# Expert layer with eight routed experts: gate and up products with the weights as the stationary operand

## The chip, the cores and the metric

The kernel runs on one core of a Trainium2 chip, in one launch. The metric is the device time of that launch in microseconds (us), as the median of several runs. All arithmetic of the stage in question is f32.

## What is computed

The reference normalises a batch of 4 x 1024 tokens of 256 features, adds a causal attention with 16 heads and a mixture of experts to the input, and returns the sum. The change touches the experts alone. Each token goes to the 2 of 8 experts that its router logits choose. An expert is a gated layer:

```
w_gate = transpose(gating_einsum, (0, 3, 1, 2)).reshape(E, F, 2 * H)        # E=8 experts, F=256, H=256
gate_out = ragged_dot(sorted_xs, w_gate, group_sizes)                       # gate and up in one product
activation = gelu(gate_out[:, 0, :]) * gate_out[:, 1, :]
expert_outputs = ragged_dot(activation, linear, group_sizes)                # down, 256 -> 256
out = sum over the token's 2 experts of weight * per_expert_scale * expert_outputs
```

## The kernel before, in words

The program is a row of stages that end in a barrier each: `project` (layer norm, q, k, v), `route` (which token goes to which expert), `attend`, `experts`, `combine` (weights the expert rows, projects the context, adds all up). The route stage sorts the 8192 pairs of token and expert into `NST` = 72 tiles of 128 rows; a tile belongs to one expert, whose number stands in `tile_expert`, in memory, because it depends on the data.

In `experts` each tile s passes through these steps, every one on its own engine, tied by semaphores:

- POOL gathers the tile's 128 rows of 256 numbers from memory by an indirect DMA (`gather`, L951) into one of `RR` = 4 buffers, 6 tiles ahead.
- TensorE (PE) transposes them in two 128x128 pieces (`rows_T`, L1028), and ACT copies the result out of PSUM (`xT_copy`, L981).
- `gate_up` (L1037): two matmuls of 512 columns into one PSUM bank, one for each half of the 256 features. The stationary operand is the transposed tile (128x128), the moving one are the expert's 512 columns of gate and up weights, addressed with the expert number read by `expert_of` (L1032, `value_load`). The result has tokens on the partitions.
- ACT computes the gelu of the gate half (`gelu`, L985), VectorE (DVE) multiplies it by the up half (L1014, `hid`).
- PE transposes `hid` in two pieces (`hidden_T`, L1044) and DVE copies them out of PSUM (L1016, `hT`).
- `down` (L1050): two matmuls of 256 columns, stationary `hT`, moving the expert's down weights, again by the expert's number.
- ACT copies the result out (`store`, L990), and POOL scatters the 128 rows to memory (`scatter`, L956).

One f32 matmul, and its weight load, shows as two records each in the trace; a transpose shows as one of each.

PE's order is written out by hand in `turn`: two reads of expert numbers, `hidden_T(s-1)`, `rows_T(s+1)`, `down(s-2)`, `gate_up(s+1)`. PE and ACT run a hardware loop (`Fori`) over four tiles a pass, DVE one over two; POOL's instructions are written out without a loop. PSUM and SBUF tiles between the engines are double buffered. SP (the DMA queue) loads the down weights (2 MB) and the first inputs of `combine` (over 4 MB) at the start of the stage, L936 to L943.

Of the kernel before, what the change touches and what calls it, by code (L numbers as in the profile page):

```python
# [894 lines left out]
def experts(nc, ins, scratch, keep, last_weights):  # L895
# [4 lines left out]
    with ExitStack() as ctx:  # L900
# [8 lines left out]
        hid = sb("hid", [P, 2, HID])  # L909
# [4 lines left out]
        hp = ctx.enter_context(nc.psum_tensor("hp", [P, 2, CH], F32))  # L914
# [7 lines left out]
        gu_ready, gate_ready, hid_ready = sem("gu_ready"), sem("gate_ready"), sem("hid_ready")  # L922
        hp_ready, hT_ready = sem("hp_ready"), sem("hT_ready")
        yp_ready, y_ready = sem("yp_ready"), sem("y_ready")
        block = ctx.enter_context(nc.Block())

        def tiles(eng, body):

            with eng.Fori(0, NST // 2) as i:
                for par in range(2):  # L930
                    body(2 * i + par, par, i)
# [44 lines left out]
        @block.scalar  # L976
        def _(act):

            def xT_copy(s, par):
                act.wait_ge(tp_ready, s + 1)  # L980
                act.activation(xT[:, par].rearrange("p a t -> p (a t)"), tp[:, par, 0:D], ACT.Copy).then_inc(xT_ready, 1)  # L981

            def gelu(s, par):
                act.wait_ge(gu_ready, s + 1)
                act.activation(gate[:, par], gu[:, par, 0:HID], ACT.Gelu_apprx_tanh).then_inc(gate_ready, 1)  # L985

            def store(s, m):
                act.wait_ge(yp_ready, s + 1)
                act.wait_ge(y_free, s + 1)
                act.activation(y[:, m], yp[:, m % 2, 0:D], ACT.Copy).then_inc(y_ready, 1)  # L990

            xT_copy(0, 0)
            gelu(0, 0)
            xT_copy(1, 1)
            gelu(1, 1)
            xT_copy(2, 0)
            with act.Fori(0, NST // RR - 1) as i:
                for j in range(RR):
                    s = RR * i + 2 + j
                    gelu(s, j % 2)  # L1000
                    xT_copy(s + 1, 1 - j % 2)
                    store(s - 2, j)
            for s in range(NST - 2, NST + 2):
                if s < NST:
                    gelu(s, s % 2)
                if s + 1 < NST:
                    xT_copy(s + 1, (s + 1) % 2)
                store(s - 2, (s - 2) % RR)
# [12 lines left out]
        def _(pe):  # L1021
            pe.wait_ge(keep["w_gu_in"], 16 * NE)

            def rows_T(s, m, i):

                pe.wait_ge(rows_in[m], 16 * (i + 1))
                for dh in range(DH):
                    last = pe.transpose(tp[:, m % 2, dh * P:(dh + 1) * P], rows[:, m, dh * P:(dh + 1) * P], keep["ident"][:, :])  # L1028
                last.then_inc(tp_ready, 1)

            def expert_of(s):
                return pe.value_load(keep["tile_expert"][0:1, ds(s, 1)], min_val=0, max_val=NE - 1)  # L1032

            def gate_up(s, par, e):
# [12 lines left out]
            def down(s, par, e):  # L1047
                pe.wait_ge(hT_ready, s + 1)
                for dh in range(DH):
                    last = pe.matmul(yp[:, par, 0:D], hT[:, par, dh], w_down[:, ds(e * DH + dh, 1)].rearrange("p a c -> p (a c)"),  # L1050
# [3 lines left out]


            rows_T(0, 0, 0)
            gate_up(0, 0, expert_of(0))
            rows_T(1, 1, 0)
            gate_up(1, 1, expert_of(1))
            hidden_T(0, 0)  # L1060
            rows_T(2, 2, 0)
            gate_up(2, 0, expert_of(2))
            pe.wait_ge(w_in, 16 * NE)

            def turn(s, j, i):

                coming, going = expert_of(s + 1), expert_of(s - 2)
                hidden_T(s - 1, (j + 1) % 2)
                rows_T(s + 1, (j + 1) % RR, i + (j + 1) // RR)
                down(s - 2, j % 2, going)  # L1070
                gate_up(s + 1, (j + 1) % 2, coming)

            with pe.Fori(0, NST // RR - 1) as i:
                for j in range(2, 2 + RR):
# [274 lines left out]
```

## Time and profile before

| what | value |
|---|---|
| time, median of 3 runs | 939.3 us (938.69, 939.3, 1016.51) |
| time of the profiled execution | 941.12 us |
| its span, first to last instruction | 939.4 us |
| stage `experts`, in the span | about 632 to 879 us |
| PE busy in the whole span | 812.5 us, 86% |
| DVE, ACT, POOL busy | 562.1, 483.2, 390.0 us |
| mean granted clock of PE | 0.937 of full speed |

The time of the profiled execution is 1.7 us above its span, which is what lies around the first and the last instruction. Times in rows are microseconds from the start of the span unless marked ns. PE busy counts matmuls, whose ends are modelled and overlap the next one's start; the distance from start to start is the firmer number. "PEld" is PE loading its stationary operand, "q" behind an engine's name its queue of register and semaphore instructions.

### The profile page before, as it was taken

How to read it: one execution, taken by the hardware profiler on the slowest of the kernel's cores; microseconds unless marked ns; L12 is line 12 of the kernel's file. 1: busy time of each engine (PE TensorE's matmuls, PEld its weight loads, DVE VectorE, ACT ScalarE, POOL GpSimd, SP SyncE). 2: the span in 40 equal slices, each digit the busy share in tenths (PEclk: the TensorE clock that was granted, in tenths of full speed). 3: DMA queues.
4: the chain of work that ended last, by engine and by line, in shares of the span. 5: the costliest groups of instructions: out<-in, count | busy, mean ns of one | idle time of the engine just before them, and what ended most of it. 6: DMA issues, size and time to landing. Idle time of an engine off the chain costs nothing. (4 is left out here: it accounts for less than half of the span.)

```text
span 939.4 us, 17505 instructions
## 1 busy us (share of the span) xinstructions
PE 812.5 (86%) x5618; PEld 426.3 (45%) x5619; DVE 562.1 (60%) x1560; ACT 483.2 (51%) x1011; POOL 390.0 (42%) x456
## 2 busy tenths in 40 slices
PE   5989601799999999999999999856999999999598
PEld 2555400134444444444444444313555656555497
DVE  4767364988888888888888888301222222222177
ACT  2333300067777777777777777852333333333374
POOL 3545340033223233322323332323666666665398
PEclk9999855589999999999999999996999999999799
DMA  4999899295555666555566600009222222222485
GB/s 157 221 263 269 213 107 121 34 253 74 62 61 57 82 81 81 67 62 61 59 82 81 81 3 3 2 6 321 86 84 84 84 84 84 84 85 78 129 245 182
DMA packets 115004, 100.32 MB, mean 107 GB/s; under 512 B 58172, under 2 KB 95676, under 8 KB 114876
## 3 DMA queue, kind: packets, MB, share of 16 engines
q1 hardware_dynamic: 105976, 80.50, 46.9%
q0 software_dynamic: 8960, 18.95, 6.4%
q8 instruction: 37, 0.61, 0.3%
q14 instruction: 31, 0.25, 0.1%
HBM read 63.89 MB, written 35.00 MB: 105 GB/s over the span
## 5 line engine op out<-in xcount | busy, mean ns | idle before, releaser
L784 ACT ACTIVATE probs<-spsum 128x512 f32<-128x512 f32 x576 | 312.1, 604 | 169.6 <-PE spsum L835 163.8
L742 DVE CUSTOM_DVE_ANT_0 junk<-mpsum,mask 128x128 bf16<-128x128 f32 (+7 forms) x512 | 360.0, 754 | 58.5 <-issue 51.7
L824 PE MATMUL mpsum<-ks,qs 102*128 102x512 bf16 (+3 forms) x768 | 183.5, 343 | 45.9 <-DVE cpsum L731 26.3
L722 POOL TENSOR_SCALAR_AFFINE_SELECT probs<-probs 128x512 f32<-128x512 f32 x128 | 78.8, 634 | 340.8 <-ACT probs L784 340.8
L835 PE MATMUL spsum<-qs,ks 105*128 105x512 bf16 (+3 forms) x768 | 199.2, 329 | 10.6 <-ACT probs L784 8.3
L855 PE MATMUL cpsum<-probs,vs 128*17 128x256 f32 (+2 forms) x2560 | 152.7, 360 | 1.5 <-POOL probs L722 0.8
L1037 PE MATMUL gu<-w_gu,xTs 128*128 x288 | 139.2, 607 | 1.7 <-ACT xTs L981 1.7
L1016 DVE COPY hT<-hp 128x256 f32<-128x256 f32 x72 | 30.6, 425 | 167.8 <-PE hp L1044 100.6
L824 PEld LDWEIGHTS mpsum<-ks,qs 102*128 102x128 bf16 x768 | 69.8, 100 | 122.5 <-DVE maxima L742 39.8
L835 PEld LDWEIGHTS spsum<-qs,ks 105*128 105x128 bf16 x768 | 67.1, 97 | 102.9 <-ACT probs L784 52.9
L956 POOL DMA_INDIRECT expert_rows<-y,places x72 | 70.7, 983 | 72.2 <-ACT y L990 42.2
L855 PEld LDWEIGHTS cpsum<-probs,vs 128*17 128x17 f32 x2560 | 59.8, 97 | 77.4 <-issue 36.4
L951 POOL DMA_INDIRECT rows<-xn_rows,places x72 | 69.3, 962 | 34.9 <-issue 20.7
L985 ACT ACTIVATE gate<-gu 128x256 f32<-128x256 f32 x72 | 27.7, 384 | 100.7 <-issue 64.0
L1050 PE MATMUL yp<-w_down,hT 128*128 x288 | 74.2, 380 | 0.4 <-issue 0.4
L1037 PEld LDWEIGHTS gu<-w_gu,xTs 128*128 128x128 f32 x288 | 52.1, 193 | 45.4 <-issue 38.5
L712 POOL DMA_INDIRECT slot_map<-entries_now,slots x64 | 61.8, 966 | 17.2 <-issue 17.2
L417 PE MATMUL qkpsum<-xT,w_qk 128*128 128x512 f32 x128 | 59.8, 612 | 4.4 <-DVE rest L359 3.3
L1014 DVE TENSOR_TENSOR hid<-gu,gate 128x256 f32<-128x256 f32 x72 | 30.2, 420 | 49.3 <-ACT gate L985 49.3
L1050 PEld LDWEIGHTS yp<-w_down,hT 128*128 128x128 f32 x288 | 49.1, 190 | 4.6 <-issue 0.9
L312 POOL TENSOR_TENSOR parts<-rest,parts 128x512 bf16<-128x512 f32 x32 | 37.0, 1157 | 32.0 <-DVE parts L361 32.0
L990 ACT ACTIVATE y<-yp 128x256 f32<-128x256 f32 x72 | 27.7, 384 | 36.2 <-issue 31.8
(124 smaller groups left out, 698.5 us busy)
## 6 DMA issues: line engine op xcount, KB each, us to landing
qk_parts<-parts SPq DMA_DIRECT2D x32, 384.0 KB, 4.4
qs<-qk_parts SPq DMA_DIRECT2D x96, 128.0 KB
ks<-qk_parts SPq DMA_DIRECT2D x96, 128.0 KB
yk<-expert_rows SPq DMA_DIRECT2D x32, 256.0 KB, 3.1
v_rows<-vt SPq DMA_DIRECT2D x32, 136.0 KB, 4.5
vs<-v_rows SPq DMA_DIRECT2D x16, 272.0 KB, 12.0
x_in<-in_x SPq DMA_DIRECT2D x8, 512.0 KB, 6.3
xn_rows<-xn SPq DMA_DIRECT2D x8, 512.0 KB, 5.8
```

Source lines behind the costliest of these rows:

```text
L417: last = pe.matmul(qkpsum[:, q % 2], w_qk[:, dh, q], xT[:, par, dh], start=dh == 0, stop=dh == DH - 1)
L712: pool.indirect_dma_start(scratch["map"], bass.IndirectOffsetOnAxis(ap=slots[:, par, k, i:i + 1].bitcast(U32), axis=0), entries[:, par, k, ...
L722: pool.affine_select(out=part, in_=part, compare_op=ALU.is_ge, fill=0.0, base=0, pattern=[[0, 4], [1, P]], channel_multiplier=-1).then_inc ...
L742: last = dve.tensor_tensor_reduce(junk[:, slot, c:c + w], mpsum[:, slot, c:c + w], keep["mask"][:, S - w:S], 1.0, 3 * NEG, ALU.add, ALU.ma ...
L784: act.activation(probs[:, u % PRING, h], spsum[:, (4 * u + h) % SRING], ACT.Exp, scale=SCALE).then_inc(exp_done, 1)
L824: last = pe.matmul(mpsum[:, slot, at + c:at + e], qs[hq][0:R_MAX, h, qt * P:(qt + 1) * P], ks[hq][0:R_MAX, h, c:e], start=True, stop=True)
L835: last = pe.matmul(spsum[:, (4 * u + h) % SRING, c:c + w], ks[hq][:, h, kt * P:(kt + 1) * P], qs[hq][:, h, q0:q0 + w], start=True, stop=True)
L855: last = pe.matmul(cpsum[32 * h:32 * h + VW, q0 % CH:q0 % CH + w], vs[hq][:, kt, h], probs[:, u % PRING, h, c:c + w], start=i == 0 and (u, ...
L951: pool.indirect_dma_start(rows[:, s % RR], None, scratch["xn"], bass.IndirectOffsetOnAxis(ap=places[:, s, 0:1].bitcast(U32), axis=0)).then ...
L956: pool.indirect_dma_start(scratch["y"], bass.IndirectOffsetOnAxis(ap=places[:, s, 1:2].bitcast(U32), axis=0), y[:, s % RR], None).then_inc ...
L1037: last = pe.matmul(gu[:, par], xT[:, par, dh], w_gu[:, ds(e * DH + dh, 1)].rearrange("p a c -> p (a c)"), start=dh == 0, stop=dh == DH - 1)
L1050: last = pe.matmul(yp[:, par, 0:D], hT[:, par, dh], w_down[:, ds(e * DH + dh, 1)].rearrange("p a c -> p (a c)"), start=dh == 0, stop=dh == ...
```

## The change

The gate and up products are turned round: the expert's weights are the stationary operand, and the transposed tile moves. The product then comes out with the hidden units on the partitions, which is what `down` wants as its stationary operand, so `hidden_T`, its PSUM tile `hp` and the copy out of it are gone, and DVE's multiply writes `hT` itself. Each tile has 8 matmuls of 128 columns in place of 2 of 512. The stationary operand is read from `w_now`, a double-buffered copy (128 x 1024 numbers) of the expert's weights, which DVE makes for each tile with an expert number that it reads itself; PE waits for it with a new semaphore. All loops are written out, addresses of expert numbers are constants, and PE's order is `gate_up(s)`, `rows_T(s+2)`, `down(s-1)`, one read of an expert number. ACT's order is `gelu(s)`, `xT_copy(s+2)`, `store(s-1)`. `down` has an explicit wait on `y_ready`. POOL and SP are as before.

```diff
-        hid = sb("hid", [P, 2, HID])
+        w_now = sb("w_now", [P, 2, DH, 2 * HID])
-        hp = ctx.enter_context(nc.psum_tensor("hp", [P, 2, CH], F32))
...
         @block.scalar
-            with act.Fori(0, NST // RR - 1) as i:
-                for j in range(RR):
-                    s = RR * i + 2 + j
-                    gelu(s, j % 2)
-                    xT_copy(s + 1, 1 - j % 2)
-                    store(s - 2, j)
...
+            xT_copy(0)
+            xT_copy(1)
+            for s in range(NST):
+                gelu(s)
+                if s + 2 < NST:
+                    xT_copy(s + 2)
+                if s >= 1:
+                    store(s - 1)
+            store(NST - 1)
 
         @block.vector
         def _(dve):
-            def body(s, par, i):
+            def weights(s):
+
+                e = dve.value_load(keep["tile_expert"][0:1, s:s + 1], min_val=0, max_val=NE - 1)
+                dve.tensor_copy(w_now[:, s % 2].rearrange("p a c -> p (a c)"), w_gu[:, ds(e * DH, DH)].rearrange("p a c -> p (a c)")).then_inc(w_ready, 1)
+
+            dve.wait_ge(keep["w_gu_in"], 16 * NE)
+            weights(0)
+            weights(1)
+            for s in range(NST):
                 dve.wait_ge(gate_ready, s + 1)
-                dve.tensor_tensor(hid[:, par], gu[:, par, HID:2 * HID], gate[:, par], ALU.mult).then_inc(hid_ready, 1)
-                dve.wait_ge(hp_ready, s + 1)
-                dve.tensor_copy(hT[:, par].rearrange("p a t -> p (a t)"), hp[:, par, 0:HID]).then_inc(hT_ready, 1)
-
-            tiles(dve, body)
+                dve.tensor_tensor(hT[:, s % 2].rearrange("p a t -> p (a t)"), gu[:, s % 2, HID:2 * HID], gate[:, s % 2], ALU.mult).then_inc(hT_ready, 1)
+                if s + 2 < NST:
+                    weights(s + 2)
 
         @block.tensor
...
+            def gate_up(s):
+
                 pe.wait_ge(xT_ready, s + 1)
+                pe.wait_ge(w_ready, s + 1)
+                for c in range(2 * HID // P):
+                    for dh in range(DH):
+                        last = pe.matmul(gu[:, s % 2, P * c:P * (c + 1)], w_now[:, s % 2, dh, P * c:P * (c + 1)],
+                                         xT[:, s % 2, dh], start=dh == 0, stop=dh == DH - 1)
+                last.then_inc(gu_ready, 1)
+
+            def down(s, e):
+                pe.wait_ge(hT_ready, s + 1)
+                if s >= 2:
+                    pe.wait_ge(y_ready, s - 1)
                 for dh in range(DH):
-                    last = pe.matmul(gu[:, par], xT[:, par, dh], w_gu[:, ds(e * DH + dh, 1)].rearrange("p a c -> p (a c)"),
-                                     start=dh == 0, stop=dh == DH - 1)
-                last.then_inc(gu_ready, 1)
-
-            def hidden_T(s, par):
-                pe.wait_ge(hid_ready, s + 1)
-                for dh in range(DH):
-                    last = pe.transpose(hp[:, par, dh * P:(dh + 1) * P], hid[:, par, dh * P:(dh + 1) * P], keep["ident"][:, :])
-                last.then_inc(hp_ready, 1)
...
-            with pe.Fori(0, NST // RR - 1) as i:
-                for j in range(2, 2 + RR):
-                    turn(RR * i + j, j, i)
...
+            rows_T(0)
+            rows_T(1)
+            going = expert_of(0)
+            for s in range(NST):
+                gate_up(s)
+                if s + 2 < NST:
+                    rows_T(s + 2)
+                if s == 1:
+                    pe.wait_ge(w_in, 16 * NE)
+                if s >= 1:
+                    down(s - 1, going)
+                    going = expert_of(s)
+            down(NST - 1, going)
```

## Rows read from the trace of the kernel before

**Rows 1.** Windows by stage: window, us, each engine's busy us, PEclk, DMA share, GB/s

```profile
653.60:867.80 214.20, 211.79 (x829) 127.11 (x829) 53.88 (x138) 79.52 (x207) 131.32 (x135) 1.00 0.27 87
879.00:939.40 60.40, 53.17 (x320) 47.93 (x320) 39.65 (x96) 35.35 (x80) 47.56 (x32) 0.90 0.70 210
```

**Rows 2.** Timeline of one turn: start, us, engine, line, operation, tiles [idle before]

```profile
672.12 0.38 PE L1044 MATMUL hp<-ident,hid 128*128 128x128 f32 x2
...
672.32 0.38 ACT L985 ACTIVATE gate<-gu 128x256 f32<-128x256 f32 x1 [1.33 <-issue]
672.34 0.38 PE L1028 MATMUL tp<-ident,rows 128*128 128x128 f32 x2
...
672.54 0.42 DVE L1016 COPY hT<-hp 128x256 f32<-128x256 f32 x1 [2.26 <-issue]
672.55 0.96 POOL L951 DMA_INDIRECT rows<-xn_rows,places  x1 [0.30 <-issue]
672.56 1.03 PE L1050 MATMUL yp<-w_down,hT 128*128 x4
672.76 0.39 ACT L981 ACTIVATE xTs<-tp 128x256 f32<-128x256 f32 x1
672.92 0.42 DVE L1014 TENSOR_TENSOR hid<-gu,gate 128x256 f32<-128x256 f32 x1
...
673.42 1.88 PE L1037 MATMUL gu<-w_gu,xTs 128*128 x4
673.62 0.38 ACT L990 ACTIVATE y<-yp 128x256 f32<-128x256 f32 x1 [0.48 <-issue]
...
674.28 0.98 POOL L956 DMA_INDIRECT expert_rows<-y,places  x1 [0.77 <-issue]
...
675.14 0.38 PE L1044 MATMUL hp<-ident,hid 128*128 128x128 f32 x2
```

**Rows 3.** Timeline of PE: a late turn, and the turns of hidden units 1 and 70

```profile
653.58 0.44 PE L1044 MATMUL hp<-ident,hid 128*128 128x128 f32 x2
...
678.49 0.43 PE L1044 MATMUL hp<-ident,hid 128*128 128x128 f32 x2 [0.17 <-issue]
...
867.81 0.38 PE L1044 MATMUL hp<-ident,hid 128*128 128x128 f32 x2
```

**Rows 4.** Timeline of weight loads, in two narrow windows, and of eight transposes in `combine`

```profile
681.89 0.19 PEld L1050 LDWEIGHTS yp<-w_down,hT 128*128 128x128 f32 x1
...
681.89 0.30 PEld L1050 LDWEIGHTS yp<-w_down,hT 128*128 128x128 f32 x2
...
903.96 1.04 PE L1164 MATMUL sumsT<-ident,ctxT 128*128 128x128 f32 x8
```

**Rows 5.** One line's instructions: count, ns min/median/max, first and last start

```profile
L1032 PEldq TENSOR_LOAD <-tile_expert x144: 295/302/494, 640.5 to 870.0; - x144
...
L1050 PEldq FUSED_REGOPS  x144: 55/60/60, 653.9 to 870.9; - x144
```

**Rows 6.** DVE copies: a row of groups by shape (busy, mean ns), and one line's durations

```profile
L346 DVE COPY xT<-tpsum 128x512 f32<-128x512 f32 x8 | 5.5, 685 | 1.9 <-PE tpsum L404 1.9
...
L361 DVE CAST parts<-rest x32: 426/428/886, 18.3 to 107.5; 128x512 bf16<-128x512 f32 x32
```

**Rows 7.** Timeline in `project`: a DVE cast beside a POOL instruction

```profile
42.35 1.16 POOL L312 TENSOR_TENSOR parts<-rest,parts 128x512 bf16<-128x512 f32 x1 [1.96 <-DVE parts L361]
...
42.90 0.89 DVE L361 CAST parts<-rest 128x512 bf16<-128x512 f32 x1
```

**Rows 8.** Timeline of PE at the start of `experts`

```profile
640.45 0.66 PE L1028 MATMUL tp<-ident,rows 128*128 128x128 f32 x2 [12.96 <-DMA rows<-xn_rows,places]
...
647.46 2.77 PE L1037 MATMUL gu<-w_gu,xTs 128*128 x3
```

**Rows 9.** Timeline at the end of `experts`

```profile
872.07 0.38 ACT L990 ACTIVATE y<-yp 128x256 f32<-128x256 f32 x1 [0.63 <-PE yp L1050]
872.97 0.96 POOL L956 DMA_INDIRECT expert_rows<-y,places  x1 [0.30 <-issue]
```

More of the change, by code:

```diff
@@ L921, in experts @@
         tp_ready, xT_ready = sem("tps_ready"), sem("xTs_ready")
-        gu_ready, gate_ready, hid_ready = sem("gu_ready"), sem("gate_ready"), sem("hid_ready")
-        hp_ready, hT_ready = sem("hp_ready"), sem("hT_ready")
+        gu_ready, gate_ready, hT_ready, w_ready = sem("gu_ready"), sem("gate_ready"), sem("hT_ready"), sem("w_now_ready")
         yp_ready, y_ready = sem("yp_ready"), sem("y_ready")
         block = ctx.enter_context(nc.Block())
[L927 to L931, printed above, removed]
         @block.sync
@@ L977, in _, with xT_copy, gelu @@
         def _(act):
-            def xT_copy(s, par):
+            def xT_copy(s):
                 act.wait_ge(tp_ready, s + 1)
-                act.activation(xT[:, par].rearrange("p a t -> p (a t)"), tp[:, par, 0:D], ACT.Copy).then_inc(xT_ready, 1)
-            def gelu(s, par):
+                act.activation(xT[:, s % 2].rearrange("p a t -> p (a t)"), tp[:, s % 2, 0:D], ACT.Copy).then_inc(xT_ready, 1)
+            def gelu(s):
                 act.wait_ge(gu_ready, s + 1)
-                act.activation(gate[:, par], gu[:, par, 0:HID], ACT.Gelu_apprx_tanh).then_inc(gate_ready, 1)
@@ L987, in store @@
-            def store(s, m):
+                act.activation(gate[:, s % 2], gu[:, s % 2, 0:HID], ACT.Gelu_apprx_tanh).then_inc(gate_ready, 1)
+            def store(s):
                 act.wait_ge(yp_ready, s + 1)
                 act.wait_ge(y_free, s + 1)
[L990 to L996, printed above, removed]
-            with act.Fori(0, NST // RR - 1) as i:
-                for j in range(RR):
-                    s = RR * i + 2 + j
-                    gelu(s, j % 2)
-                    xT_copy(s + 1, 1 - j % 2)
-                    store(s - 2, j)
@@ L1003, in _ @@
[L1003 to L1008, printed above, removed]
+                act.activation(y[:, s % RR], yp[:, s % 2, 0:D], ACT.Copy).then_inc(y_ready, 1)
+            xT_copy(0)
[6 more added lines that the diff above has]
+                    store(s - 1)
@@ L1020, in _, with rows_T @@
+                if s + 2 < NST:
+                    weights(s + 2)
         @block.tensor
         def _(pe):
-            pe.wait_ge(keep["w_gu_in"], 16 * NE)
-            def rows_T(s, m, i):
-                pe.wait_ge(rows_in[m], 16 * (i + 1))
+            def rows_T(s):
+                pe.wait_ge(rows_in[s % RR], 16 * (s // RR + 1))
                 for dh in range(DH):
-                    last = pe.transpose(tp[:, m % 2, dh * P:(dh + 1) * P], rows[:, m, dh * P:(dh + 1) * P], keep["ident"][:, :])
+                    last = pe.transpose(tp[:, s % 2, dh * P:(dh + 1) * P], rows[:, s % RR, dh * P:(dh + 1) * P], keep["ident"][:, :])
@@ L1029, in rows_T @@
                 last.then_inc(tp_ready, 1)
             def expert_of(s):
-                return pe.value_load(keep["tile_expert"][0:1, ds(s, 1)], min_val=0, max_val=NE - 1)
-            def gate_up(s, par, e):
+                return pe.value_load(keep["tile_expert"][0:1, s:s + 1], min_val=0, max_val=NE - 1)
+            def gate_up(s):
                 pe.wait_ge(xT_ready, s + 1)
-                for dh in range(DH):
-                    last = pe.matmul(gu[:, par], xT[:, par, dh], w_gu[:, ds(e * DH + dh, 1)].rearrange("p a c -> p (a c)"),
-                                     start=dh == 0, stop=dh == DH - 1)
-                last.then_inc(gu_ready, 1)
@@ L1041, in hidden_T @@
-            def hidden_T(s, par):
-                pe.wait_ge(hid_ready, s + 1)
-                for dh in range(DH):
-                    last = pe.transpose(hp[:, par, dh * P:(dh + 1) * P], hid[:, par, dh * P:(dh + 1) * P], keep["ident"][:, :])
-                last.then_inc(hp_ready, 1)
[L1047 to L1050, printed above, removed]
+                pe.wait_ge(w_ready, s + 1)
@@ new lines, in gate_up @@
+                for c in range(2 * HID // P):
[7 more added lines that the diff above has]
+                    pe.wait_ge(y_ready, s - 1)
+                for dh in range(DH):
+                    last = pe.matmul(yp[:, s % 2, 0:D], hT[:, s % 2, dh], w_down[:, ds(e * DH + dh, 1)].rearrange("p a c -> p (a c)"),
@@ L1051, in down @@
                                      start=dh == 0, stop=dh == DH - 1)
                 last.then_inc(yp_ready, 1)
[L1056 to L1071, printed above, removed]
@@ L1073, in _ @@
-            with pe.Fori(0, NST // RR - 1) as i:
-                for j in range(2, 2 + RR):
-                    turn(RR * i + j, j, i)
-            turn(NST - 2, 2, NST // RR - 1)
-            hidden_T(NST - 2, 0)
-            down(NST - 3, 1, expert_of(NST - 3))
-            hidden_T(NST - 1, 1)
-            down(NST - 2, 0, expert_of(NST - 2))
-            last_expert = expert_of(NST - 1)
-            pe.wait_ge(y_ready, NST - 2)
-            down(NST - 1, 1, last_expert)
+            rows_T(0)
```

## The prediction

> **What bounds the kernel now.** I read the page first, to find the stage, then windows by stage, then the timeline of one turn. Between its third and its last-but-one turn the expert stage takes 214.2 us, at the full granted clock (1.00, which is 2.4 GHz), with PE busy 211.8 us of it; DVE has 54, ACT 80, POOL 131, and the DMA engines a share of 0.27 [rows 1]. So PE sets the pace, and only what PE does, or what would push another engine above PE, changes the time.
>
> One turn shows what PE does [rows 2]. From start to start: hidden units transposed 0.22 us (672.12 to 672.34), rows transposed 0.22, `down` 0.86 (672.56 to 673.42), `gate_up` 1.72 (673.42 to 675.14). That is 3.02 us with no gap. Over many turns it is more: the hidden units of tile 1 are transposed at 653.58 and those of tile 70 at 867.81 [rows 3], so 69 turns take 214.23 us, **3.105 each**. The 5.9 us over 69 x 3.02 are stalls like the one at 678.49, where the same transposes start 3.35 us after the ones at 675.14 [rows 2, 3]; one such turn, with a smaller delay (0.05) in the next, comes in every four. I take it for the turn of PE's four-tile loop; where it is not, the 5.9 us may stay.
>
> **What the change does to PE, per turn.**
>
> Removed: two transposes of hidden units, 0.22 us.
>
> Kept: rows 0.22, `down` 0.86.
>
> Turned round: `gate_up` has 8 matmuls of 128 columns instead of 2 of 512, thus 16 pairs of load and matmul records instead of 4. The columns streamed are the same, 8 x 128 = 2 x 512. A record of 512 columns takes 1.72 / 4 = 0.43 us and one of 256 takes 0.86 / 4 = 0.215, so time is proportional to columns, and 128 would take 0.108. The new question is the load. No row has a full f32 load in front of a 128-column f32 matmul. From below: transposes have a 128x128 f32 load each for 128 columns, and eight in a row take (1.04 - 0.27) / 7 = 0.11 us each [rows 4] (0.27 is how long one lasts, 0.38 for two that start 0.11 apart). Their load may be the cheaper kind. From above: an f32 load of `down` lasts 0.19 us. But two of them last 0.30 together [rows 4], so the second starts 0.11 after the first: a load needs 0.11 of the port and the rest is latency under the next. I take 0.11, since it is the same kind of load. `gate_up` becomes 16 x 0.11 = 1.76 us, with ends of 1.74 (16 x 0.109, nothing lost) and 16 x 0.19 = 3.04.
>
> Sum: 1.76 + 0.22 + 0.86 = **2.84 us a turn**. Against 3.105 this is 0.265 x 69 = **18.3 us** saved, of which 5.9 is the loop's stalls, 15.2 the transposes (0.22 x 69), less 2.8 for 16 pairs at 0.11 (0.04 x 69).
>
> **Who must stay under 2.84 us.** Let 0 be the end of `gate_up(s)` on PE; gelu starts 0.2 after it (`gate_up` ends at 672.12, gelu is at 672.32) [rows 2].
>
> *ACT*: gelu 0.2 to 0.58, the row copy to 1.0, then `store(s-1)`, about 0.2 after `down(s-1)` ends at 0.22 + 0.86 = 1.08, so to 1.65. 1.15 us of work, and `gate_up(s+2)` wants the copied rows only at 2.84 + 1.08 = 3.9. No cost.
>
> *DVE*: the multiply (0.42) replaces a multiply and a copy (0.42), and ends at about 1.0. `down(s)` wants it at 2.84 + 0.22 = 3.06, so 2 us of cover; before, the transposes stood in between. Then it reads the expert number. On PE's queue the memory read takes 0.30 [rows 5] and with its register steps I estimate 0.7, partly under the multiply. Copying 1024 numbers: a PSUM source costs 0.42 for 256 [rows 2] and 0.685 for 512 [rows 6], so 0.16 fixed and 1.03 ns each; an SBUF source, 512 in 0.43, is then half of that each, 0.52 ns [rows 6]. So 0.69 us, at most 0.16 + 1.05 = 1.22. The copy runs from about 1.4 to 2.1 (2.6), and `gate_up(s+2)` wants it at 3.9. Behind it on DVE is only the next multiply, at 2.84 + 0.6. DVE's turn is 0.42 + 0.7 + 0.69 = 1.8 us. No cost, with 1.3 to 1.8 us to spare.
>
> *PE's own queue*: before, two reads of expert numbers a turn ran while `gate_up` streamed; now it is one, against 22 pairs of records. A register step of `down` takes 0.06 [rows 5], and `down` still has two. The cover is the work queued in front of the array: the next `gate_up` waits for nothing that is late, so its loads are queued during `down` and the previous `gate_up`. I cost it at nothing; if the queue held less than 0.7 us of work, each turn would lose up to 0.7.
>
> *POOL*: gather 0.96 and scatter 0.98, with 0.30 before the gather [rows 2]. Before the scatter 0.77 stands, but there it waits for `y` (673.62 + 0.38 = 674.00, scatter at 674.28); back to back I take 0.30. Minimum 0.96 + 0.98 + 0.60 = 2.54, under 2.84 by 0.3. Its writes to SBUF buffers are freed by `rows_T(s+2)`, earlier than before. A gather for tile s+6 is issued about 3.2 us after the end of `gate_up(s+1)`, and its rows are wanted at the end of `gate_up(s+4)`, 5.3 us later.
>
> **Ends of the stage.** Start: PE's first transposes wait for rows until 640.45, and at half clock a `gate_up` record takes (2.77 - 1.06) / 2 = 0.855 us [rows 8]. Before, three `gate_up`s are done at 653.58. After: rows of tiles 0 and 1 by about 642.2 (0.96 + 0.30 apart, as POOL issues them [rows 2]), two `gate_up`s of 3.4 and three pairs of row transposes of 0.43, the first `down` of 1.7 and a `gate_up` between 1.8 and 3.4: 653 to 655. I take no change, with +-1.5. End: before, the last `gate_up` ends at 867.81 and the last scatter starts at 872.97 [rows 3, 9], 5.2 later, after transposes, copy and two `down`s in sequence. After: down of tile 70 0.86, the multiply ready at 1.0, `down` 0.86 more with some 0.2 of start, copy out 0.2 + 0.38, scatter 0.3 later: 3.0. That saves **2.2 us**.
>
> **Sum.** 18.3 + 2.2 = 20.5 us off the profiled execution: 941.1 - 20.5 = 920.6, span 918.9. The median of the runs stands 1.8 below the profiled execution, so it comes to **918.8 us**. Bounds of this case: at 2.82 a turn 1.4 less, with a quicker start 915.5; at 2.90 (small stalls at each wait) 4 more, and 925 with a slow start too.
>
> **Rivals.**
>
> *A port between DVE and POOL.* In `project` a DVE cast from SBUF to SBUF lasted 0.89 instead of 0.43 while POOL had an instruction from 42.35 to 43.51; it ended 0.28 after POOL's [rows 7]. So such a DVE copy and POOL exclude each other at least once, and the new copy is of this kind. No row has it beside an indirect DMA. If it holds for the whole instruction, POOL's turn and the copy are in series: 0.96 + 0.30 + 0.98 + 0.69 = 2.93, or 3.16 with another 0.23 of waiting before the scatter. That gives 918.8 + 69 x (0.09 to 0.32) = 925 to 941, most likely about 932. Against it: the copy (1.4 to 2.1) falls in POOL's idle time, as the gather ends near 3.2 + 0.96 - 2.84 = 1.3 and the scatter starts near 1.9. Chance 0.17.
>
> The Trainium skill ("SBUF — State Buffer", section "SBUF: two separate sides") says that a DVE copy that uses both ports, f32 SBUF to SBUF among them, keeps POOL from writing the descriptors of its DMAs. By that rule every turn in which the two meet would carry up to the whole copy; it speaks against this change, and is the mechanism of this rival.
>
> *Loads don't hide* (the other side: slower). If a load takes port time while a 128-column f32 matmul streams, a pair costs up to 0.19 and a turn 3.04 + 1.08 = 4.12, which is 70 us more than before: 1007. It decides from 0.129 a pair on (no gain: 0.11 + 20.5 / (16 x 69)) and is slower by 2% from 0.146. Against it are the two loads 0.11 apart, though there the matmul beneath was a transpose. Chance 0.09; a middle value of 0.15 gives 963.
>
> *PE's queue, or fetching code that is no longer a loop.* PE now takes some 50 instructions each 2.84 us, all new ones. For it: stalls with `issue` as releaser exist [rows 3]. Against: `combine` is written out too, with DMA engines busier (0.70), and PE is busy 53 of 60 us [rows 1]. If the 0.085 a turn of stalls stays, or grows to 0.25: 925 to 936. Chance 0.12.
>
> Elsewhere 0.02.
>
> **How the numbers follow.** The forecast has 0.60, and the predicted time is its 918.8. A 2% change is 18.8 us, thus 920.5; about what a measurement can tell from no change. The forecast's case lies on both sides of that line, about two thirds below it: faster 0.41. Within 2%: a third of the forecast, both stall cases, small overruns of loads: 0.49. Slower: loads 0.08 and the rest, 0.10. The range from 915.5 to 936 holds the forecast, most of the port's and of the queue's cases, 0.8 in all; the likeliest case alone spans 915.5 to 925.
>
> **What would show it.** `gu` matmuls 0.11 apart and 16 a turn; starts of `down` 2.84 apart with no turn of 3.35; the full clock throughout; DVE copies of 0.69 us; indirect DMAs still 0.96 and 0.98. Copies or DMAs stretched in some turns would show the port, gaps on PE ended by `issue` the queue, loads spaced 0.15 or more the second rival. The prediction is wrong if `w_now` is ever what `gate_up` waits for, or if POOL has no idle time left.

## The result, and where the time stands

The changed kernel takes 946.99 us (median of 6 runs, 945.03 to 949.02), the kernel before beside it 941.25 (6 runs). One of these six, 1016.51 us, was a slow run and is left out of the ratio. The ratio is **1.0068, 95% interval 1.0046 to 1.0090**: slower by 0.7%, within the 2% that count as no change. The forecast was 918.8 with a range of 915.5 to 936. It is wrong in sign and outside its range.

The profiled execution has a span of 943.3 us (939.4 before). Here is the window of the changed kernel's expert stage; it is as long as the first of [rows 1] but for 0.2 us. Columns: window, us, busy us of each engine with the number of instructions, granted clock, DMA share, GB/s.

```profile
652.00:866.00 214.00, 200.08 (x1466) 184.08 (x1465) 73.10 (x133) 66.81 (x199) 136.16 (x132) 0.99 0.28 89
```

PE is idle for 13.9 us of 214, where before it was idle for 2.4 [rows 1]. `combine` is as long as before (60.3 us against 60.4). The granted clock is 0.99 against 1.00: from 757.3 on it stood at half (1.2 GHz) for 3.4 us. PE had been idle for 2.0 us before `down` of that turn at 756.38, and the `gate_up` at half clock took 3.44 us, 1.65 more than the others. The rest of the time went inside the turns too, at the full clock. Two rows of PE's timeline, the `gate_up` of tiles 3 and 71, give their mean:

```profile
654.04 1.95 PE L1028 MATMUL gu<-xTs,w_now 128*128 128x128 f32 x16
...
872.37 1.95 PE L1028 MATMUL gu<-xTs,w_now 128*128 128x128 f32 x16
```

218.33 us over 68 turns are **3.211 each**; before it was 3.105 [rows 3]. Yet a turn in which nothing is late is short. PE's rows of one, answering to [rows 2]:

```profile
761.91 1.95 PE L1028 MATMUL gu<-xTs,w_now 128*128 128x128 f32 x16
...
763.70 0.38 PE L1016 MATMUL tp<-ident,rows 128*128 128x128 f32 x2
...
763.91 1.03 PE L1037 MATMUL yp<-w_down,hT 128*128 x4
...
764.78 1.95 PE L1028 MATMUL gu<-xTs,w_now 128*128 128x128 f32 x16
```

761.91 to 764.78 is 2.87 us, of which `gate_up` has 1.79, or 0.112 a record. The forecast said 2.84. What the 0.34 between 2.87 and 3.21 consists of is seen in other turns, such as this one, from tile 10 on:

```profile
676.34 0.38 PE L1016 MATMUL tp<-ident,rows 128*128 128x128 f32 x2
...
677.43 1.95 PE L1028 MATMUL gu<-xTs,w_now 128*128 128x128 f32 x16
...
679.21 0.38 PE L1016 MATMUL tp<-ident,rows 128*128 128x128 f32 x2
680.12 0.38 ACT L977 ACTIVATE gate<-gu 128x256 f32<-128x256 f32 x1 [4.72 <-PE gu L1028]
680.40 0.38 ACT L973 ACTIVATE xTs<-tp 128x256 f32<-128x256 f32 x1
680.54 0.42 DVE L1006 TENSOR_TENSOR hT<-gu,gate 128x256 f32<-128x256 f32 x1 [5.00 <-ACT gate L977]
680.66 0.39 ACT L982 ACTIVATE y<-yp 128x256 f32<-128x256 f32 x1
680.93 0.41 ACT L977 ACTIVATE gate<-gu 128x256 f32<-128x256 f32 x1
...
681.11 1.13 PE L1037 MATMUL yp<-w_down,hT 128*128 x4 [1.52 <-DVE hT L1006]
```

Read it from the bottom. `down` starts at 681.11, 1.9 us after the transposes instead of 0.22, and waited for the multiply. The multiply waited for gelu. Gelu waited for `gate_up` of tile 10, which ended at 676.34 or so: the row transposes follow it without a gap. In [rows 2] gelu starts 0.2 us after that point; here it is 3.8, with ACT idle for 4.72. Then two gelus, two row copies and a store come one behind another, for the updates of two `gate_up`s, two transposes and a `down` reach ACT all at once. The trace also has the moment of each semaphore's update. PE's semaphores of this stage have none between 675.0 and 680.1, and then five within 0.3 us: 680.10 (`gate_up` of tile 10), 680.14 (transposes), 680.20 (`down` of tile 9), 680.36 (`gate_up` of tile 11), 680.40 (transposes). So it is the updates that come late, and not ACT. I call a turn late where gelu starts over 0.9 us after the last `gate_up` record. By the records' times 36 of 72 turns are late, by 0.95 to 4.3 us, and the mean delay of all is 1.26 us instead of 0.20. Gelu's wait for PE from 660 to 865; columns: engine and line, what it waited for, us in total, times, longest:

```profile
ACT gate L977 <- PE gu L1028: 64.1, 29, 5.4
```

In a good turn gelu waits some 1.4 us; 5.4 is a late one. Another 39.8 us, in 11 waits of up to 4.1, stand under "remote", which is this view's word for a wait that it can put down to no update at all (the trace holds 67 of the 72 updates of `gate_up`).

The balance: turns cost 68 x (3.211 - 3.105) = 7.2 us more. `gate_up` of tile 3 starts 0.9 earlier (654.04 against 654.93, which is 653.58 [rows 3] and 1.35 later), and the end of the stage saves 2.1 (3.0 against 5.2 [rows 3, 9]):

```profile
874.15 1.03 PE L1037 MATMUL yp<-w_down,hT 128*128 x4
...
877.17 0.96 POOL L948 DMA_INDIRECT expert_rows<-y,places  x1 [0.33 <-ACT y L982]
```

The last `gate_up` ends at 874.15 and the last scatter starts 3.0 later, as forecast. Together 7.2 - 0.9 - 2.1 = 4.2, against 3.9 between the spans.

### The profile page after: what moved, and what is told of

It is laid out like the page before. It is cut to its first block and busy times, and to the rows that moved or that the text cites. A ratio compares the mean times of both kernels' runs of the same rounds, so it can differ in the third digit from the quotient of the medians.

```text
span 943.3 us, 18424 instructions
## 1 busy us (share of the span) xinstructions
PE 804.4 (85%) x6338; PEld 493.2 (52%) x6338; DVE 585.5 (62%) x1560; ACT 473.4 (50%) x1011; POOL 397.9 (42%) x456
## 5 line engine op out<-in xcount | busy, mean ns | idle before, releaser
L1028 PEld LDWEIGHTS gu<-xTs,w_now 128*128 128x128 f32 x1152 | 141.1, 195 | 9.1 <-issue 4.5
L1028 PE MATMUL gu<-xTs,w_now 128*128 128x128 f32 x1152 | 145.0, 280 | 0.5 <-issue 0.3
L824 PEld LDWEIGHTS mpsum<-ks,qs 102*128 102x128 bf16 x768 | 69.8, 100 | 122.3 <-DVE maxima L742 39.8
L1006 DVE TENSOR_TENSOR hT<-gu,gate 128x256 f32<-128x256 f32 x72 | 30.5, 424 | 141.3 <-ACT gate L977 87.4
L948 POOL DMA_INDIRECT expert_rows<-y,places x72 | 75.0, 1042 | 70.6 <-ACT y L982 56.7
L943 POOL DMA_INDIRECT rows<-xn_rows,places x72 | 72.9, 1012 | 33.2 <-issue 20.7
L1037 PE MATMUL yp<-w_down,hT 128*128 x288 | 76.1, 387 | 12.2 <-DVE hT L1006 10.3
L999 DVE COPY w_now<-w_gu 128x1024 f32 x72 | 50.5, 702 | 57.9 <-issue 57.7
L1016 PE MATMUL tp<-ident,rows 128*128 128x128 f32 x144 | 28.3, 279 | 17.3 <-DMA rows<-xn_rows,places 15.9
```

Of the source, the lines that this page charges most:

```text
L824: last = pe.matmul(mpsum[:, slot, at + c:at + e], qs[hq][0:R_MAX, h, qt * P:(qt + 1) * P], ks[hq][0:R_MAX, h, c:e], start=True, stop=True)
L943: pool.indirect_dma_start(rows[:, s % RR], None, scratch["xn"], bass.IndirectOffsetOnAxis(ap=places[:, s, 0:1].bitcast(U32), axis=0)).then ...
L948: pool.indirect_dma_start(scratch["y"], bass.IndirectOffsetOnAxis(ap=places[:, s, 1:2].bitcast(U32), axis=0), y[:, s % RR], None).then_inc ...
L1028: last = pe.matmul(gu[:, s % 2, P * c:P * (c + 1)], w_now[:, s % 2, dh, P * c:P * (c + 1)], xT[:, s % 2, dh], start=dh == 0, stop=dh == DH ...
L1037: last = pe.matmul(yp[:, s % 2, 0:D], hT[:, s % 2, dh], w_down[:, ds(e * DH + dh, 1)].rearrange("p a c -> p (a c)"), start=dh == 0, stop=d ...
```

## The experiments

After the session of the result the kernels were run in five more. All kernels of a session ran on one chip, with the kernel before run among them; ratios are always to that one. Its median differs from session to session, and in the end that turned out to matter most: 939.78 in the first, 933.36 in the second, 946.64 in the third, 932.46 in the fourth, 940.79 in the fifth.

**First session: the port, the rows, the expert numbers, the matmuls' width.**

```
a_nocopy        in dve, for each tile:  -  if s + 2 < NST: weights(s + 2)
                in pe:                  -  pe.wait_ge(w_ready, s + 1)
                                        +  pe.wait_ge(w_ready, min(s + 1, 2))
a_ring8         - RR = 4 row buffers, AHEAD = 6      + RB = 8, AHEAD = 10 (rows only)
a_static_down   - return pe.value_load(keep["tile_expert"][0:1, s:s + 1], ...)
                + return s % NE
b_split         the kernel before, gate_up: 2 matmuls of 512 columns -> 8 of 128:
                + for c in range(2 * HID // P): ... w_gu[:, ds(e * DH + dh, 1), P * c:P * (c + 1)]
```

> The changed kernel without VectorE's copies of the weights after the first two tiles (all tiles then use the weights of the experts of tiles 0 and 1; the multiply stays). In the changed kernel a turn without stalls is 2.87 us, near the forecast 2.84, but in about 19 of 72 turns the semaphore updates of PE's finished matmuls show 2 to 4 us after the matmuls, and the mean turn is 3.21. Theory copy (VectorE's copy, or the port it shares with POOL, starts the stalls): turns of 2.87 throughout, about 922 us. Theories rows wait, PE read, instruction rate: stalls stay, 940 to 947 us; indirect DMAs stretched from 0.98 to 1.0-1.7 us are back at 0.98 in any case.

Measured 943.71, ratio 1.0052 (1.0037 to 1.0066); mean turn 3.200, 37 late turns. The copies did lengthen POOL's indirect DMAs. The scatters of the changed kernel, and then of this one (count, ns least/median/most, first and last start):

```profile
L948 POOL DMA_INDIRECT expert_rows<-y,places x72: 958/985/1697, 652.0 to 877.2; - x72
```

```profile
L948 POOL DMA_INDIRECT expert_rows<-y,places x72: 958/987/1002, 650.1 to 874.5; - x72
```

Without copies the longest is 1.00 us instead of 1.70, and the turn is as slow as ever. So copies and scatters do get in each other's way, and it costs nothing that shows here (3.200 against 3.211 a turn).

> The changed kernel with 8 row buffers and gathers 10 tiles ahead, so that PE's queue, which runs up to a turn ahead of the array, never waits for rows in front of `down`. Theory rows wait (PE's queue waits for the rows of tile s+2 until after gate_up(s) has started, loses its lead, and the updates come late): no late updates, turns of 2.87, about 922 us. Theories copy, PE read, instruction rate: 940 to 947 us, with the same late updates though the queue is ahead.

Measured 938.76, ratio 0.9987 (0.9972 to 1.0002); mean turn 3.133, 30 late turns. More depth in the rows left 30 of the late turns.

> The changed kernel with PE not reading expert numbers: the down weights of tile s are those of expert s mod 8. That takes 0.7 us a turn and two register steps from PE's queue. Theory PE read (finished matmuls' updates are held while PE's queue reads memory and then refills): no late updates, about 922 us. Others: 940 to 947 us.

Measured 938.49, ratio 0.9999 (0.9973 to 1.0025); mean turn 3.131, 28 late turns. The read of the expert number in PE's queue isn't it either. These two have 0.07 us a turn less than `a_nocopy`; the late turns stay.

> The kernel before, loops and orientation kept, with gate_up in 8 matmuls of 128 columns (the same transposed tile loaded 8 times). Records per turn rise from 24 to 48 as in the changed kernel, the array's time from 3.02 to 3.06 us a turn. Theory instruction rate (some 15 records of loads and matmuls per us for long hold the updates): late updates here too, mean turn 3.3 or more, 955 us or more. Other theories: mean turn about 3.14, 941 to 945 us, no late updates.

Measured 983.80, ratio 1.0463 (1.0415 to 1.0510); mean turn 3.763, no late turn. That met no expectation. Each of the eight matmuls has its own register steps in PE's queue, and PE waits for its queue: it is busy 157.93 of 180 us in the window from 660 to 840, and the transposes of hidden units stand idle for 22.3 us there, 48 times, with `issue` as what ended it. This kernel has 48 records a turn, matmuls and loads together, against the changed kernel's 44, at a slower rate (12.8 a us, where 44 in 2.87 us are 15.3) and without lateness.

**Second session: fewer records, smaller records, a slower turn, more depth.**

```
a_cols256    gate_up: 4 matmuls of 256 columns (moving operand w_gu[:, dh, 0:2 * P])
a_m64        gate_up: w_now[:, s % 2, dh, P * c:P * c + P // 2], 64 output partitions;
             gelu, multiply and down on 64 partitions
a_down384    down: 384 columns a matmul instead of 256 (w_gu[..., 0:P + D])
a_deep       gu, gate, hT, xTs, w_now in 3 buffers, rows in 8;
             - rows_T(s + 2) ... down(s - 1, going)    + rows_T(s + 3) ... down(s - 2, going)
```

> The changed kernel with gate_up as 4 matmuls of 256 columns instead of 8 of 128 (stationary the first two column pieces of w_now, moving a fixed piece of the weights; the values are not the layer's). Array time 1.72 us as before, records of loads and matmuls in a turn 28 instead of 44. Theory backlog (PE's finished instructions report at a limited rate; 44 records in 2.87 us are too many, so the updates fall behind by up to 4 us): no late updates, turns near 2.8, about 918 us. Theory latency (something else in the order of the changed kernel delays the updates): 938 to 947 us.

Measured 909.78, ratio 0.9752 (0.9718 to 0.9786); turn 2.818, no late turn. As the last kernel of the second session shows, nothing was late in it, so neither this run nor the next two tell the theories apart.

> The changed kernel with 64 of the 128 weight columns loaded for each gate_up matmul, so that half of the units is computed (gelu, multiply and down use 64 partitions). Same number of records, same columns streamed, each load of gate_up about half as long. Backlog by number of records: late updates and 938 to 947 us stay. Backlog by the time of full f32 loads: no late updates, about 918 us.

Measured 946.76, ratio 1.0148 (1.0114 to 1.0182); turn 3.311 in nearly every turn, none late. It is inconclusive for another reason too: a new cost came in. In PE's timeline `gate_up` has 1.89 us instead of 1.79, the transposes 0.37 instead of 0.21 and `down`, by the turn before, 1.06 instead of 0.87 (starts at 760.31, 761.37, 763.26 and 763.63).

> The changed kernel with 384 instead of 256 columns in down's matmuls (moving operand from the gate and up weights; not the layer's values). Same 44 records, array time of a turn 2.87 + 0.43 = 3.30 us. Backlog theory: 44 records in 3.30 us are fewer than the 44 in 3.13 to 3.21 that the chip sustained, so no late updates, no stalls, 69 x 0.09 to 0.17 us above the changed kernel: 950 to 957 us. Theory latency: late updates stay and add their stalls, 965 us or more.

Measured 943.10, ratio 1.0109 (1.0073 to 1.0144); turn 3.292, none late. That does not show that the longer turn is what helps: 44 records in 2.87 us were not late in the second session either.

> The changed kernel with more slack: gate_up's PSUM tile, gate, hT, xT and w_now in three buffers, rows transposed three tiles ahead, down two tiles behind, 8 row buffers. An update may be 5 us late before PE waits for it. If late updates are a delay that comes and goes (at most about 4 us), PE never waits: turns of 2.87, about 920 us. If they are a backlog with a limited rate, PE is held in the end as before, mean turn 3.13 to 3.2, 936 to 944 us.

Measured 915.99, ratio **0.9810 (0.9783 to 0.9837)**, which beats both kernels; turn 2.862, not one late. I took this for proof that the waits of `down` one tile behind make the lateness. But the changed kernel had not run in that session.

**Third session: the two halves of the deep version, the change again, and loops alone.**

```
c_down2      down(s - 2) for down(s - 1); gu, gate, hT in 3 buffers; nothing else
c_rows3      rows_T(s + 3), xTs and w_now in 3 buffers, rows in 8; down(s - 1) stays
after_again  the changed kernel
b_unrolled   the kernel before:
             - with pe.Fori(0, NST // RR - 1) as i:    + for i in range(NST // RR - 1):
             (and likewise on ACT and DVE)
```

> The changed kernel with one part of the deep version alone: the down product runs two tiles behind gate_up instead of one (gu, gate and hT in three buffers); rows, rows transposed and weight copies stay as in the change. Nothing is left out. Theory T (TensorE's updates get late where its queue stands at the wait for hT(s-1) just behind gate_up(s)): no late updates, turn 2.87 us, ratio to the kernel before 0.975 to 0.985. Rival R (what helped the deep version was that rows, transposed rows and weight copies were one tile further ahead): turn stays at 3.15 to 3.21 us with 25 to 37 turns of late updates, ratio 0.998 to 1.008.

Measured 955.47, ratio 1.0076 (1.0049 to 1.0103). One late turn only, but the median turn went to 3.12 us, the mean to 3.24. A scatter comes a turn later, and the gather behind it too, and PE's transposes now wait for rows: 5.4 of the 9.2 us that they stand idle for, from 660 to 840. That the rows make the whole difference is argued, not shown.

> The other part of the deep version alone: rows gathered ten tiles ahead in eight buffers, transposed rows and weight copies three tiles ahead; the down product stays one tile behind. Nothing is left out. Theory T: late updates stay, turn 3.1 to 3.2 us, ratio 0.995 to 1.007. Rival R: no late updates, turn 2.87 us, ratio 0.975 to 0.985. If both this kernel and the one with the down product two tiles behind reach 2.87, either slack is enough and the cause is the sum of short waits; if neither does, both are needed.

Measured 951.49, ratio 1.0046 (1.0028 to 1.0063); mean turn 3.230, 30 late turns. Neither half gives what the whole gave, though the whole had run in another session.

> The changed kernel as it is, beside the others on this chip. By its first runs: ratio to the kernel before 1.005 to 1.009, turn 3.2 us with about 36 turns of late updates. If the lateness were a matter of the chip and not of the kernel, a turn of 2.87 us and a ratio near 0.98 could come out.

Measured 951.90, ratio 1.0054 (1.0038 to 1.0071); mean turn 3.228, 34 late turns.

> The kernel before with its loops over tiles written out, nothing else changed: the part of the change that is 'no loops' alone. By the prediction's step for the loops (5.9 us of stalls of the loop over 69 turns): 5 to 7 us less, ratio 0.993 to 0.995. Rival (written-out code costs TensorE its queue or its code loading): late updates as in the changed kernel or stalls of 1 us and more, ratio 1.00 to 1.02.

Measured 937.92, ratio **0.9898 (0.9875 to 0.9920)**, 8.7 us less. Every turn has 3.019 us, none is late, and PE has no gap at all (window, busy us as above):

```profile
660.00:840.00 180.00, 180.00 (x717) 110.96 (x716) 45.35 (x120) 68.92 (x180) 115.42 (x119) 1.00 0.29 92
```

So the stalls of [rows 3] were the loops', PE's, ACT's and DVE's taken together. In one session the two parts of the change now stand side by side: written-out loops -8.7 us, the rest of it 951.90 - 937.92 = +14.0.

**Fourth session: the tight wait alone, the deep version without its copies, the loop.**

```
c_down2r   c_down2 with rows in 8 buffers, AHEAD = 10
c_tight    a_deep, in down(s - 2):
           - pe.wait_ge(hT_ready, s + 1)    + pe.wait_ge(hT_ready, min(s + 2, NST))
c_loops    the changed kernel, PE's turn in a loop, order and waits kept:
           + with pe.Fori(0, NST // RR - 2) as i:
           +     for j in range(4, 4 + RR): turn(RR * i + j, j, i)
```

> The changed kernel with the down product two tiles behind gate_up (gu, gate and hT in three buffers) and the rows gathered ten tiles ahead in eight buffers; transposed rows and weight copies stay two tiles ahead. Nothing is left out. With the down product two behind alone, there was 1 late update instead of 34, but the usual turn went to 3.12 us, and the trace put that down to the rows: a scatter is now one turn later, and the gather behind it too. Theory T (the tight wait of the down product makes the late updates, the gathers made the rest): turn 2.87 us, no late updates, ratio 0.978 to 0.985. Rival (transposed rows and weight copies three ahead are needed too): ratio 0.99 to 1.01.

Measured 914.24, ratio 0.9811 (0.9789 to 0.9832); turn 2.865, none late.

> The deep version (ratio 0.981, turn 2.87 us) with one wait moved: the down product of tile s-2 waits for hT of tile s-1 instead of its own, at the same place in TensorE's order. Work, buffers and transfers are the same, nothing is left out. Theory T (a wait in TensorE's queue for a product that its own preceding gate_up has only just made possible brings the late updates): late updates return, 20 or more, turn 3.0 to 3.25 us, ratio 0.995 to 1.01. Rival D (the depth of the buffers is what helps, however the waits stand): turn 2.87 us, ratio 0.978 to 0.985.

Measured 914.64, ratio 0.9806 (0.9783 to 0.9828); turn 2.862, none late. The tight wait is back, the lateness is not: my theory T falls as the one cause. What the tight wait does in a session in which updates come late, this run cannot tell.

> The changed kernel with TensorE's work in a loop of four tiles a pass, as the kernel before has it; order, waits and the other engines' code are those of the change, and nothing is left out. Theory C (the late updates come with fresh code that TensorE has to load all the time, where its queue stands close behind the array): no late updates, usual turn 2.87 to 2.95 us, with a stall at each pass of the loop of 0.3 to 1 us, ratio 0.985 to 0.995. Theory T alone (order and waits make them, whatever the code): 25 to 37 late updates stay, ratio 1.005 to 1.02.

Measured 915.60, ratio 0.9825 (0.9804 to 0.9846); turn 2.869, none late. Nothing in it is deeper than in the changed kernel. Taken alone it would make written-out code the culprit. But laid out by session, late turns stood only where the kernel before took 939 us or more, and never where it took 932 or 933. The fifth session was made for that.

**Fifth session: the kernel or the chip.**

> The changed kernel as it is, beside the next two on one chip. The late updates were seen only in calls in which the kernel before took 939 to 947 us, and none of eight kernels showed them in the two calls in which it took 932 to 933 us; the changed kernel has not run beside those. Theory K (the kernel's order or code makes them on any chip): 25 or more late updates, ratio 1.004 to 1.009. Theory H (the chip decides): on a chip where the kernel before takes 939 us or more the same 1.004 to 1.009, on one where it takes 932 to 934 us no late updates, turn 2.87 us, ratio 0.978 to 0.985.

> The changed kernel with the down product two tiles behind and rows ten tiles ahead, again (0.981 beside a kernel before of 932 us). Nothing is left out. Theory K: ratio 0.978 to 0.985 wherever it runs. Theory H: the same only where the kernel before takes 932 to 934 us; where it takes 939 us or more, late updates or late rows, turn 3.0 to 3.2 us, ratio 0.99 to 1.01.

> The changed kernel with TensorE's work in a loop, again (0.9825 beside a kernel before of 932 us). Nothing is left out. Theory K, in the form that written-out code is the condition: ratio 0.98 to 0.985 wherever it runs. Theory H: the same only where the kernel before takes 932 to 934 us; where it takes 939 us or more, 25 or more late updates as in the changed kernel, ratio 1.004 to 1.02.

Measured, beside a kernel before of 940.79: the changed kernel 947.48, ratio 1.0067 (1.0044 to 1.0090), 36 late turns; `down2r_again` 948.81, ratio **1.0069** (1.0046 to 1.0093), 30 late; `loops_again` 948.10, ratio **1.0082** (1.0054 to 1.0109), 28 late. The last two are, word for word, kernels that had 0.9811 and 0.9825 one session before. Here are the same windows of the same kernel (the one with the loop), first from the fourth session, then from the fifth:

```profile
660.00:840.00 180.00, 180.00 (x1382) 173.54 (x1382) 70.51 (x126) 65.37 (x188) 131.65 (x124) 1.00 0.29 91
```

```profile
660.00:840.00 180.00, 166.47 (x1210) 154.25 (x1210) 59.98 (x109) 54.75 (x164) 115.12 (x110) 0.98 0.25 80
```

PE without a gap and 1382 matmul records, against 13.5 us of gaps and 1210. And gelu's waits from 660 to 860, in the same order:

```profile
ACT gate L977 <- PE gu L1028: 91.0, 65, 1.4
```

```profile
ACT gate L977 <- PE gu L1028: 86.4, 36, 5.5
```

In the fourth session all 65 waits of gelu are 1.4 us, one per turn. In the fifth there are 36 that the view can assign, up to 5.5. The code is the same, and the DMA engines are less busy where PE is late. The granted clock (1.00 and 0.98) can't be the cause: the changed kernel beside it has 1.00 in this window and is as late. **For these two kernels it is the session that decides, and it is worth 2.6% of the time.** That much of theory H holds. That the chip decides is not shown: by the chips' numbers on record, number 3 had the first session (939.78, late updates) as well as the fourth (932.46, none). Either the number does not name one chip, or the same chip was different 37 minutes later.

`down2r_again` shows also that the lateness finds another way where `down` has a turn more of cover. There PE waits for the transposed rows and for the copied weights (from 660 to 860), which in the changed kernel cost it 2.1 and 0.2 us:

```profile
PEld gu L1030 <- ACT xTs L974: 20.5, 11, 2.7
PE gu L1030 <- DVE w_now L1001: 16.3, 10, 2.3
```

How the kernels stand by mean turn (from the records, `gate_up` of tile 3 to that of tile 71):

| session (kernel before) | kernels with 44 records in 2.87 us | others |
|---|---|---|
| 941.25 | changed kernel 3.211 | |
| 1 (939.78) | `a_nocopy` 3.200, `a_ring8` 3.133, `a_static_down` 3.131 | `b_split` 3.763 |
| 3 (946.64) | changed kernel 3.228, `c_rows3` 3.230 | `c_down2` 3.240, `b_unrolled` 3.019 |
| 5 (940.79) | changed kernel 3.231, `down2r_again` 3.219, `loops_again` 3.234 | |
| 2 (933.36) | `a_deep` 2.862 | `a_cols256` 2.818, `a_down384` 3.292, `a_m64` 3.311 |
| 4 (932.46) | `c_down2r` 2.865, `c_tight` 2.862, `c_loops` 2.869 | |

Where updates come late, the means lie between 3.13 and 3.24 whatever the waits and the depth are; elsewhere they are the sum of PE's own work. The nine cases with late updates and the four without, in the middle column, don't overlap.

The difference shows in the attention stage too, where the code is the same in all kernels. The longest wait of `probs` for its scores, from 200 to 600 us, is 1.0 us in all seven traces of the second and fourth sessions and 1.7 to 2.0 in the thirteen others, those of the kernel before, of `b_split` and of `b_unrolled` among them. Here `c_tight`, then `after_third`:

```profile
ACT probs L784 <- PE spsum L835: 91.0, 148, 1.0
```

```profile
ACT probs L784 <- PE spsum L835: 98.2, 141, 2.0
```

From the first score matmul to the last the stage takes 426.9 to 427.4 us in the seven and 432.7 to 435.1 in the thirteen. These 6 to 8 us are most of the 7 to 8 us by which the kernel before stands higher in the first and fifth sessions than in the fourth, and half of the third session's 14, and they come before the experts begin. So the sessions differ whatever kernel runs, and the kernel's part is how much the experts lose by it. The kernel before was profiled only in a session of the first kind.

**What stays open.** Why PE's updates come late in some sessions was not settled. It isn't the copies, the rows, the expert read or the written-out loop of PE. The depths that were tried in such a session and kept the 2.87 us (`a_ring8`, `c_rows3`, `down2r_again`) did not remove it; the full depth of `a_deep` was not tried in one. Whether it is the chip, its state at the time or what else ran on it is not on record. Nor is it certain that the report alone is late: the ends of matmul records are modelled. That the next records start in their usual step speaks for the report. A backlog in what PE reports, which builds up above some rate of records, would fit the table: 48 in 3.76 us (`b_split`) and 24 in 3.02 (`b_unrolled`) were never late, `c_down2` with 44 in a median 3.12 once, those with 44 in 2.87 in 28 to 37 turns of 72. That is argued, not shown; `a_cols256` (28 records in 2.82), which could have told it, ran only where nothing is late. The changed kernel itself didn't run there: that it would reach 0.98 is inferred from `c_loops` (its order, waits and depth) and `c_tight` (written out, deeper).

## Why the prediction was wrong

*The turn's arithmetic: right.* 16 records of 0.11, rows 0.22 and `down` 0.86 made 2.84; 2.87 was measured, as 0.112 x 16 = 1.79, 0.21 and 0.87. The rival that loads don't hide is out.

*The loop's stalls: right, and too small.* I took 5.9 us of them for PE's loop; `b_unrolled` gained 8.7 (7.6 to 11.8 by its interval). Its turns have the 3.019 of [rows 2], so 5.9 are in them, and the rest isn't placed. A loop alone does not bring them: `c_loops` has one on PE and turns of 2.869, though in a session in which the kernel before was not profiled.

*Start and end of the stage: right.* They take 0.9 us and 2.1 us less, where the forecast had no change +-1.5, and 2.2. (The lower end of the range is 918.8 - 1.4 - 1.5 = 915.9 by its terms, not 915.5.)

*The copy: right.* 0.69 forecast, 0.694 the median, and `gate_up` waited for it once in the stage, 0.2 us. By its own list of signs that already spoke against the prediction, but it is not what made the time.

*The port: real, without a price.* The Trainium skill ("SBUF — State Buffer", section "SBUF: two separate sides") says that a DVE copy on both ports keeps POOL from writing its descriptors. The trace agrees as far as it can show it: scatters of up to 1.70 us where copies run, of 1.00 where they don't. But POOL's idle time took it, as argued against that rival, and `a_nocopy` has the same turn. (The sum of that rival has only one of POOL's two pauses of 0.30; with both it is 3.23 a turn, thus 946 us. That this is near the measured time is chance, since the time is the same without the copies.)

*The step that failed* is in "Who must stay under 2.84 us": "gelu starts 0.2 after it", and with it the "2 us of cover" of the multiply, and "*PE's own queue* ... I cost it at nothing". I had taken 0.2 from one good turn of a kernel with 24 records a turn and treated it as a constant. With 44 records a turn, in the sessions in which the kernel before took 939 us or more, it was not: in the changed kernel's first trace it is 0.2 to 0.7 in half of the turns and 0.95 to 4.3 us in the other half, a mean of 1.26, and 2 us of cover don't hold 4. The term mis-sized is the turn: 2.84 forecast, 3.211 measured; 68 x 0.37 = 25 us, of 28.2 between 918.8 and 946.99. The turn's own 0.03 is 2 us of these, the late updates 23, with the 1.7 us of the `gate_up` at half clock among them. The rival on PE's queue came nearest (925 to 936, chance 0.12), for another reason and too small: PE isn't short of instructions, what it has done is reported late.

*What it would have been elsewhere.* In the fourth session the kernel with the change's order and waits took 0.9825 (`c_loops`). 918.8 is 0.978 of 939.3. The turn of the forecast is what was measured there. That does not make the forecast right: it named no condition under which the updates would come in time.

## What to carry to other kernels

When a change raises the number of matmul records per microsecond, do not take the delay from PE's last matmul to its reader from one good turn: give it a range and a price, for every product that PE waits for again soon. That more cover repairs it is not shown: with `down` a turn further behind, the wait moved to the rows and the weights, and the time stayed (`down2r_again`). Run such a change in more than one session, beside a kernel of known time, and look at a stage that the change leaves alone, before believing either sign: here, the same code stood at 0.981 and at 1.007. And take the parts of a change one by one: writing out the loops was worth 1% alone, in the session in which the whole was a loss.

## What the runs showed of the hardware that I had not expected

- Updates of PE arriving 1 to 4 us after the work's records, several at once, in some sessions and not in others, at the full clock (above).
- Matmuls with 64 weight columns, or 64 rows, among others with 128 cost more, not less: 3.31 us a turn instead of 2.87 (`a_m64`).
- Eight register-addressed matmuls of 128 columns in a turn left PE waiting for its queue: 3.68 us in the median turn of `b_split`, against 3.02 with two of 512.
- Written-out code was fetched in more pieces (packets on the first instruction queue over the whole run: 37 in the kernel before, 50 in the changed one, 46 in `b_unrolled`, 51 in `c_tight`), and neither `b_unrolled` nor `c_tight` had a gap on PE for it between 660 and 840 us.
